# GpSimd's wait between blocks of scattered rows: for the block before the last one, instead of the last one

## The reference

```
x = x + ga * attention(layernorm(x) * (1 + ca) + sa)      # 16 heads of 16, causal
h = layernorm(x) * (1 + cb) + sb
scores = sigmoid(h @ gate_w.T)                            # 16 experts in 4 groups of 4
keep the 2 best groups of each token; of their 8 experts the best 4, weights cw (0 elsewhere)
y = sum over experts e of cw[:, e] * ((silu(h @ Wg[e].T) * (h @ Wu[e].T)) @ Wd[e].T)
y = y + (silu(h @ Ws_g.T) * (h @ Ws_u.T)) @ Ws_d.T        # the shared expert, twice as wide
x = x + gb * (h + y)
```

## Time and profile before

| what | value |
|---|---|
| median of 3 runs | 2289.07 us (2283.73 to 2300.91) |
| the profiled execution's own time | 2295.76 us |
| its span | 2293.9 us |
| mean granted TensorE clock in it | 0.931 |
| PE busy | 2093.4 us (91%) |
| DVE busy | 1768.3 us (77%) |
| ACT busy | 1439.4 us (63%) |
| POOL busy | 518.1 us (23%) |
| POOL, scatter of the rows (L1241), 64 DMAs | 67.6 us |

### The profile page before, as it was taken

How to read it: one execution, slowest core, us unless ns; L and a number is a source line. 1 busy time by engine, 2 the same in 40 slices (tenths; PEclk the granted TensorE clock), 3 DMA queues, 4 the chain that set the end, 5 groups by cost and what they waited for, 6 DMA issues and landing times. The chain is left out here.

```text
span 2293.9 us, 43529 instructions
## 1 busy us (share of the span) xinstructions
PE 2093.4 (91%) x17338; PEld 1091.1 (48%) x17338; DVE 1768.3 (77%) x2212; ACT 1439.4 (63%) x2798; POOL 518.1 (23%) x772
## 2 busy tenths in 40 slices
PE   7689999999999999999999999999885959999994
PEld 5233333334444443444444433333365748787883
DVE  6476799999999878899999987776358636666666
ACT  5234577778888877678888888888732323333331
POOL 2000001100110100110111010000163646666661
PEclk9755799999999999999999999999976879999997
DMA  6815011111611111521111011000074323333336
GB/s 232 241 29 65 29 34 39 53 36 34 102 51 34 44 35 39 82 54 34 44 49 60 25 41 37 23 14 12 2 260 186 130 76 110 115 114 113 115 114 243
DMA packets 120813, 180.75 MB, mean 79 GB/s; under 512 B 15793, under 2 KB 80306, under 8 KB 119842
## 3 DMA queue, kind: packets, MB, share of 16 engines
q1 hardware_dynamic: 111904, 154.45, 23.7%
q0 software_dynamic: 6720, 19.01, 2.3%
q10 hardware_dynamic: 1986, 4.51, 0.5%
HBM read 99.92 MB, written 77.60 MB: 77 GB/s over the span
## 5 line engine op out<-in xcount | busy, mean ns | idle before, releaser
L775 DVE TENSOR_REDUCE mx<-S 128x2 f32<-128x1024 f32 (+3 forms) x1152 | 1279.7, 1134 | 206.1 <-PE S L688 131.8
L756 ACT ACTIVATE prob<-ST 128x512 f32<-128x512 f32 (+3 forms) x2304 | 1169.5, 559 | 360.0 <-PE ST L709 315.5
L723 PE MATMUL O<-prob,V 128*17 128x256 f32 (+1 forms) x8704 | 690.6, 391 | 0.3 <-POOL prob L666 0.3
L688 PE MATMUL S<-K,Q 48*128 48x512 f32 (+3 forms) x2304 | 573.9, 496 | 31.4 <-DVE mx L775 20.6
L709 PE MATMUL ST<-Q,K 49*128 49x512 f32 (+3 forms) x2304 | 493.5, 425 | 36.3 <-ACT prob L756 30.8
L688 PEld LDWEIGHTS S<-K,Q 48*128 48x128 f32 x2304 | 225.3, 192 | 472.6 <-issue 297.0
L666 POOL TENSOR_SCALAR_AFFINE_SELECT prob<-prob 128x512 f32<-128x512 f32 x128 | 81.4, 636 | 1217.6 <-ACT prob L756 1217.6
L709 PEld LDWEIGHTS ST<-Q,K 49*128 49x128 f32 x2304 | 225.3, 192 | 137.7 <-ACT prob L756 105.0
L723 PEld LDWEIGHTS O<-prob,V 128*17 128x17 f32 x8704 | 145.6, 96 | 288.9 <-issue 279.9
L1575 ACT ACTIVATE sg<-hg 128x512 f32<-128x512 f32 x92 | 55.2, 600 | 156.9 <-PE hu L1504 152.9
L1683 DVE TENSOR_TENSOR alo<-sg,ahi 128x512 fp32r<-128x512 f32 x92 | 88.1, 958 | 68.1 <-ACT ahi L1579 63.6
(11 more groups left out here) (238 smaller groups left out, 1765.4 us busy)
## 6 DMA issues: line engine op xcount, KB each, us to landing
cwb<-cwt SPq DMA_DIRECT2D x76, 256.0 KB, 4.9
lists<-wbd SPq DMA_DIRECT2D x132, 138.0 KB, 2.2
Q<-qs SPq DMA_DIRECT2D x192, 64.0 KB, 2.4
xs<-lists SPq DMA_DIRECT2D x19, 552.0 KB
K<-ks SPq DMA_DIRECT2D x18, 512.0 KB, 15.6
qs<-hl SPq DMA_DIRECT2D x16, 512.0 KB, 4.5
ks<-hl SPq DMA_DIRECT2D x16, 512.0 KB, 4.4
wraw<-in_wcat SPq DMA_DIRECT2D x54, 128.0 KB, 2.1
```

What stands on the lines that cost most here:

```text
L688: ins = pe.matmul(out[:, ab, 0:w], Q[g, n % QR, p, r * P:(r + 1) * P], K[G % 2][g, p, c * BW:c * BW + w], start=True, stop=not diag)
L723: ins = pe.matmul(O[32 * a:32 * a + VC, c0:c1], V[:, G, k, VC * a:VC * (a + 1)], prob[:, s % NP, a, c0:c1], start=s in FIRST and h == 0, s ...
L756: act.activation(prob[:, s % NP, 2 * p + ab, c0:BW], ST[u % ST_BANKS][:, c0:BW], ACT.Exp).then_inc(s_exp, 1)
L775: dve.tensor_reduce(mx[:, n % 2, a:a + step + 1:step, c], S[slot % S_RING][:, :, 0:w], AX_X, ALU.max).then_inc(s_free, 1)
```

## The change

The wait ahead of block n of the scatter is for block n - 2, where it was for block n - 1. Block 1 has no wait any more. All 64 DMAs, their order, their semaphores and all who wait for those are as before.

```diff
 def scatter(pool, t, d, g):
     for n in range(QT * g, QT * (g + 1)):
-        if n and n % TPB == 0:
-            pool.wait_ge(t["s_sent"][n // TPB - 1], 16 * TG * TPB)
+        if n >= 2 * TPB and n % TPB == 0:
+            pool.wait_ge(t["s_sent"][n // TPB - 2], 16 * TG * TPB)
         for k in range(TG):
             pool.indirect_dma_start(d["lists"], bass.IndirectOffsetOnAxis(ap=t["rows"][:, n, k:k + 1], axis=0),
                                     t["xe"][:, n, :], None).then_inc(t["s_sent"][n // TPB], 16)
```

## The result

The change makes the kernel slower. Five runs of the changed kernel have a median of 2331.19 us (2303.85 to 2344.78), five of the kernel before 2290.17 us (2283.73 to 2300.91); the ratio is 1.0172, with a 95% interval of 1.0121 to 1.0224. A kernel's medians are over all its runs, ratios leave out runs in a slower state that the chip falls into now and then, so the two can differ a little. Forecast were 2275.9 us and a range of 2268 to 2286.

What follows compares the result with a forecast made beforehand. GpSimd's scatter was taken to set the start of the routed tiles. Seven shortened pauses won 13.2 us, all other terms nothing: 2289.07 - 13.2 = 2275.9 us, range 2268 to 2286.

Steps and rivals of the forecast that it cites:

- What bounds the kernel: Scatter at L1241: GpSimd's sequence sets the start of the routed tiles; PE idles 19.95 us; gains there should reach the end.
- The ordinary pause: Seven pauses ahead of scatter blocks, 15.3 us, shrink to 0.305 us each: 13.2 us won.
- The new waits fulfilled in time: Scatter's waits for block n - 2: already fulfilled when asked, with seven issues (9 us) in hand; costed at nothing.
- the long pause ahead of block 4: Scatter's 4.30 us pause, from a late landing beside a 512 KB load: goes whole; 12.7 us total gain at the low end.
- More DMAs in flight: Scatter's queue: a third or fourth DMA in flight only beside a 512 KB load; costed at zero, bound 2.0 us.
- What is late next: SP's first routed load also needs s_pre 6, capping the gain at 15.2 us; begin(5) and PE's shared blocks don't move.
- The scatter against DVE: Scatter issues stretched beside DVE's begin operations, 6.2 us now: up to 5 us won or 4 lost, taken as no change.
- The rival "slower": GpSimd writes out the 56 issues behind block 0 more slowly when earlier DMAs aren't drained: 2334 us; chance 4%.
- The rival "the shared blocks take over": SP waits for s_pre instead of the scatter: gain 15.2, with fast PE restart 17 us, 2272 to 2274; chance 12%.
- PE's clock: PE's slow start at the first routed tile stays, costed at nothing; were it gone, 2 us would be won.
- What would show it: Profile after: gaps about 0.3 us, no L1241 idleness ended by own DMAs, last issue about 1841, PE's wait about 6.8 us.

Runs made afterwards that it cites:

- halves_lag1: Kernel before, with groups of four DMAs instead of eight, each waiting for the group just sent: 2303.12 us, ratio 1.0056 to the kernel before.
- halves_lag2: Changed kernel, with groups of four DMAs, each waiting for the group before the last (at most eight under way): 2331.2 us, ratio 1.0188 to the kernel before.
- timed_pause: Changed kernel plus two small powers nobody needs on GpSimd ahead of every block but the first: 2285.11 us, ratio 0.9993 to the kernel before.

## Why the prediction was wrong, step by step

- **What bounds the kernel** was right for the kernel before: the scatter's sequence sets the start of the routed tiles, and what is won or lost there arrives at the end. The stretch behind the first routed tile took 432.4 us before and 432.7 after, with 32 us more ahead of it; halves_lag1 loses 13.8 us in the stretch (first R +120.0) and 4.6 more behind it in its profile, and is measured at 1.0056, or 13 us (3 to 22 by the interval).
- **The ordinary pause** (13.2 us) was right as a sum on GpSimd: the seven pauses are gone, the issues keep 0.96 us, and the scatter is 10.0 us shorter although it now waits 7.5 us for DVE (13.2 - 7.5, and 4.2 less stretching of the issues).
- **The new waits fulfilled in time, and the long pause ahead of block 4**: right, no idle time ended by own DMAs is left. What stands ahead of block 4 now is a wait for DVE, which I hadn't seen as late next.
- **More DMAs in flight, costed at zero**: the price came out right for the wrong question. halves_lag2 caps the number and loses 1.9%, timed_pause caps it no more than the change does and loses nothing. What counted was the distance in time from one DMA to the next, over more than some ten of them.
- **The failed step** is that of *What is late next*: "it doesn't move, nor do PE's shared blocks, which hang on nothing of the scatter". By semaphores and operands that is so, but for the wait of `begin(5)` for block 5, which had landed long before. In the runs DVE's routing and PE's and ACT's shared blocks moved by 26 and about 20 us: beside indirect DMAs every 1.26 us, more than about ten of them, other engines' instructions start late. `begin(5)` ended 133.6 us behind the first issue instead of 86.2. That the issues themselves run at full rate, as they did, says nothing of the others.
- **The scatter against DVE**: the sum took no change, in bounds of 5 won to 4 lost. The 64 issues took 63.4 us instead of 67.6, 4.2 won, as the late shared blocks left only two `begin`s within the scatter. The other direction, the scatter against DVE's short operations, stood in no sum.
- **The rival "slower"** had the right side, at 4%, and the wrong mechanism and price: issues written out more slowly, 2334 us. The issues didn't get slower; that the time after is near it is chance. Its counter-argument, "seven issues already follow each other undrained at 0.96 us", held for runs of eight, and the change makes runs of 32. The rows of before contain no run longer than eight, so they could price an issue in one but not its effect on others; that was the place for a bound on both sides, and for a chance above 4%.
- **The rival "the shared blocks take over"** (12%) came true by its own mark: SyncE issues the load of the first routed tile 1.09 us behind the end of `begin(5)`, 1863.23 + 1.23. So `s_pre`, and no longer the scatter, sets the start of the routed tiles. But the rival had the shared blocks stay where they were and a gain of 15 to 17 us; they came 47 us late.

```profile
1863.23 1.23 DVE L1626 TENSOR_TENSOR big<-big,xs 128x1024 f32<-128x1024 f32 x1
```

```profile
1865.55 0.42 SPq L1354 DMA_DIRECT2D xs<-lists  x1
```

- **PE's clock**, costed at nothing: right, the eight transposes of the first routed tile take 1.97 us after an idle time of 4.80 us as they did after 19.95.
- **What would show it**: short gaps and no own share of L1241 held, the last issue came at +88.9 where the sum had +85.7 (7.5 of waiting for DVE, less 4.2 of stretching), and PE's wait fell to 4.80, for another reason than the one given: the shared blocks came late. The marks of a gain were all on the path that the change touches. None asked whether others stay where they are.

The Trainium skill ("SBUF — State Buffer", Who interferes with whom) was cited for GpSimd's reads beside a `tensor_tensor`. The stalls here are of another kind: they hit L1161 and L1555 between instructions, not within one (0.16 and 0.59 us as before). On its inference that writing descriptors is free of such contention the rows speak against it: the nine issues of 1.3 us or more, seven before and two after, all begin within a `tensor_tensor` of DVE's with both inputs in SBUF, though most issues beside one keep their 0.96 us.

## What to carry to other kernels

A pause on a queue that seems to cost its length may be what keeps other engines prompt, at least in executions that are recorded: before taking it out, look at the longest run and the highest mean rate that the trace has shown so far, and treat what goes beyond as a new operation without a price. When engines that share nothing with the changed one start late at unchanged durations ("issue" or "remote" in many places at once), vary that engine's rhythm, with a timed pause in place of the wait; that is one run, and it tells rhythm from dependence. Count the records too: where a trace lacks signals that must have been given, ask what an execution without records would do. Idle time of PE ahead of a late transfer is worth filling only if what is taken from behind it was on the path there.

## What the runs showed of the hardware

- GpSimd's indirect DMAs, one each 1.26 us, hold up other engines from about the eleventh on: DVE's operations of 0.09 and 0.16 us start in steps of 0.7 us instead of 0.07 us apart, and ACT stands idle for up to 15.5 us before work that PE had ended long before (24.4 with an issue each 1.20 us). It was over within 5 us of the end of the last issue. Whether executions without records show it was not tested.
- By the mean distance over the first 32: from 1.46 us up there is none of it; at 1.43 a short crawl, at 1.41 with rests some late signals; at 1.34 and below it is there in full or nearly. With small operations behind each DMA it is there at 1.27 and 1.31 us from one to the next, and not at 1.83 and 1.99.
- It goes neither by bytes (128 or 1104 a row) nor by rows (64 or 128), and plain DMAs don't do it, from GpSimd (0.54 us each) or SyncE (0.59 us apart in the mean), 64 of them with the same signals.
- The transfers don't back up meanwhile: first packet 0.6 us behind the issue, last 2.1 us behind its start. The trace loses updates of the scatter's semaphores beside indirect DMAs: 604 of 1024 held before, 204 after, all with plain ones.
- An indirect DMA takes GpSimd 0.96 us to write out, but up to 2.00 us where it begins beside one of DVE's `tensor_tensor`s with both inputs in SBUF (1818.72 beside L1622 at 1818.67).
